# A four-layer convolution megakernel: filler products in TensorE's gaps, the last sums of one branch layer moved to VectorE, fewer TensorE taps in one chunk

## What is computed

```
x = x + L0(_gn(x))   # attention over the 4096 positions, softmax, value = key
x = x + L1(_gn(x))   # weights from a 128->16->9*128 net, 9 dilated taps: (wgt * patches).sum(axis=2)
x = x + L2(_gn(x))   # depthwise 7x7 (49 taps), layer norm over channels, 128->512 gelu ->128
x = x + L3(_gn(x))   # deformable 3x3 convolution, batch norm, relu
```

## Time and profile before

| | us |
|---|---|
| median of 3 runs | 4083.04 |
| the profiled execution, own time | 4088.41 |
| its span | 4086.7 |
| TensorE busy | 3426.9 |
| VectorE busy | 3225.1 |
| GpSimd busy | 2259.4 |
| ScalarE busy | 1954.3 |
| mean granted TensorE clock, share of full | 0.909 |

### The profile page before, as it was taken

How to read it: one execution, slowest core, us unless ns; L and a number is a source line. 1 busy time by engine, 2 the same in 40 slices (tenths; PEclk the granted TensorE clock), 3 DMA queues, 4 the chain that set the end, 5 groups by cost and what they waited for, 6 DMA issues and landing times. The chain is left out here.

```text
span 4086.7 us, 79072 instructions
## 1 busy us (share of the span) xinstructions
PE 3426.9 (84%) x28785; PEld 2168.6 (53%) x28785; DVE 3225.1 (79%) x6715; ACT 1954.3 (48%) x4385; POOL 2259.4 (55%) x2502
## 2 busy tenths in 40 slices
PE   4999968889999977979999976979999996883555
PEld 1666623447677742337767752335777762343444
DVE  5999867579999956659999957749999976755665
ACT  2444422346666632336666652345666653232333
POOL 3454550168878742038888835017887855006775
PEclk9999988989999988979999988989999998895556
DMA  1000002255555412055555521044555530127775
GB/s 50 9 12 12 27 16 51 66 154 149 154 154 148 125 37 50 1 170 153 151 150 152 150 61 43 8 129 142 156 152 146 155 95 18 44 63 209 220 218 175
DMA packets 219936, 426.59 MB, mean 104 GB/s; under 512 B 27825, under 2 KB 126540, under 8 KB 217512
## 3 DMA queue, kind: packets, MB, share of 16 engines
q0 software_dynamic: 92160, 302.06, 26.1%
q1 hardware_dynamic: 127346, 119.53, 10.2%
q10 hardware_dynamic: 54, 0.01, 0.0%
HBM read 340.77 MB, written 60.65 MB: 98 GB/s over the span
## 5 line engine op out<-in xcount | busy, mean ns | idle before, releaser
L1657 POOL TENSOR_TENSOR xl<-pt 128x192 bf16<-128x192 f32 (+1 forms) x1024 | 688.8, 674 | 425.0 <-PE bank L551 209.1
L878 ACT ACTIVATE pt<-bank 128x512 f32<-128x512 f32 x1024 | 608.8, 595 | 576.4 <-PE bank L520 344.9
L1646 POOL DMA_INDIRECT G<-patch_table,idx x576 | 593.9, 1031 | 162.8 <-issue 110.8
L551 PEld LDWEIGHTS bank<-vt,pt 128*128 128x128 bf16 x8192 | 550.0, 98 | 243.1 <-ACT pt L878 3.9
L1209 DVE TENSOR_REDUCE mxc<-bank 128x1 f32<-128x512 f32 x896 | 607.6, 679 | 37.4 <-PE bank L478 35.0
L551 PE MATMUL bank<-vt,pt 128*128 128x129 bf16 (+1 forms) x8192 | 634.3, 221 | 1.1 <-ACT osb L886 1.1
L1269 DVE TENSOR_TENSOR xl<-pt 128x320 bf16<-128x320 f32 (+1 forms) x1024 | 501.1, 490 | 72.3 <-PE bank L551 54.3
L551 PE MATMUL bank<-vt,xl 128*128 128x129 bf16 x4096 | 401.9, 221 | 12.7 <-DVE xl L1269 12.6
L1623 POOL TENSOR_TENSOR rs<-ve,mhalf 128x4 f32<-128x4 f32 x32 | 34.3, 1071 | 623.2 <-ACT ve L1005 623.2
L478 PE MATMUL bank<-reg,qh 128*128 128x512 bf16 x896 | 345.2, 386 | 12.0 <-DVE mxc L1209 8.5
L691 PE MATMUL bank<-reg,val 128*32 128x512 bf16 x3264 | 275.0, 399 | 65.4 <-DMA G<-xl 65.4
(11 more groups left out here) (248 smaller groups left out, 7020.2 us busy)
## 6 DMA issues: line engine op xcount, KB each, us to landing
patch_table<-valt SPq DMA_DIRECT2D x64, 512.0 KB, 7.0
G<-patch_table,idx POOLq DMA_INDIRECT x576
x_cur<-in_x SPq DMA_DIRECT2D x4, 2048.0 KB, 9.3
xl<-in_x SPq DMA_DIRECT2D x32, 256.0 KB
attn_out<-ob SPq DMA_DIRECT2D x32, 256.0 KB, 2.3
x_store<-x_cur SPq DMA_DIRECT2D x4, 2048.0 KB, 6.2
xr<-x_store SPq DMA_DIRECT2D x32, 256.0 KB
out<-fo SPq DMA_DIRECT2D x32, 256.0 KB
```

The costliest lines, as they stand in the source:

```text
L551: last = mm(O[t // 2][:, c0:c0 + width], image[:, at % ring, t * 128:(t + 1) * 128], vhl[:, values, st, 0:width], start=(st == 0 and part ...
L878: A(pt[:, at % PT_RING, :], ST[at % ST_RING] if n else ST_FIRST[at % 3], ACT.Exp, scale=SCALE).then_inc(s["exp_done"], 1)
L1646: g.indirect_dma_start(out=patches(j, k), out_offset=None, in_=table[:], in_offset=bass.IndirectOffsetOnAxis(ap=idx[:, j * K1 + k:j * K1 + ...
L1657: g.tensor_tensor(pl[:, at % PL_RING, 0:stop], pt[:, at % PT_RING, 0:stop], ph[:, at % PT_RING, 0:stop], ALU.subtract).then_inc(s["pl_p"], 1)
```

## The change

It has three parts. `keep_busy(bank, count)` lets TensorE multiply a constant (the bf16 identity) with another constant (512 columns of the layer-1 weights) `count` times, into a PSUM bank that nobody reads at that time; such calls are put around every group norm, behind the first products of layer 1 and in `step(8)` of layer 2. For the last chunk of layer 1 GpSimd keeps one addition alone and VectorE does the other three. In the first chunk of layer 2 TensorE does 27 taps in place of 34 and VectorE 22 in place of 15. In the diff the pieces stand in this order: TensorE (`keep_busy`, `layer1`, `layer2`, `sample`), VectorE (`layer1`, `layer2`), GpSimd (`layer1`).

```diff
-PE_TAPS = 34
+PE_TAPS, PE_TAPS_FIRST = 34, 27
...
+            def keep_busy(bank, count):
+
+                for _ in range(count):
+                    mm(P[bank], identb[:], l1w2_s[:, 0:CH // C, :], start=True, stop=True)
...
             def layer1(n):
...
                     mm(ST[c % 2][:], l1w1_s[:], rows(c), start=True, stop=True).then_inc(s["t_ps"], 1)
+                keep_busy(5, 20)
                 wait_alone(pe, s["tl_rdy"], NCH * n + 1)
...
                 def step(c, conv=True, norm=True, result=True):
...
+                    pe_taps = PE_TAPS if c else PE_TAPS_FIRST
...
                     if conv:
                         taps(12, 22)
+                    elif norm:
+                        keep_busy(2, 7)
...
-                        taps(25, PE_TAPS).then_inc(s["dwp"], 1)
+                        taps(25, pe_taps).then_inc(s["dwp"], 1)
+                    elif norm:
+                        keep_busy(2, 3)
...
             def sample(n, dcn):
+                if dcn:
+                    keep_busy(2, 18)
                 group_norm(4 * n)
+                if dcn:
+                    keep_busy(2, 8)
                 attention(n, dcn)
+                keep_busy(5, 50)
                 group_norm(4 * n + 1)
+                keep_busy(5, 8)
                 layer1(n)
+                keep_busy(5, 6)
                 group_norm(4 * n + 2)
+                keep_busy(5, 55)
                 layer2(n)
+                keep_busy(5, 6)
                 group_norm(4 * n + 3)
+                keep_busy(5, 28)
                 layer3_prepare(n)
...
                     if c >= 2:
                         stats(c - 2)
+                p, part = prod[(NCH - 1) % 3], pool_part[:, (NCH - 1) % 2, :]
+                dve.drain()
+                v.tensor_tensor(p[:, 4:6, :], p[:, 4:6, :], p[:, 6:8, :], ALU.add)
+                dve.drain()
+                v.tensor_tensor(p[:, 4, :], p[:, 4, :], p[:, 5, :], ALU.add)
+                dve.drain()
+                dve.wait_ge(s["l1x"], n + 1)
+                dve.wait_ge(s["l1a"], NCH * n + NCH - 2)
+                v.tensor_tensor(part, p[:, 4, :], p[:, 8, :], ALU.add).then_inc(s["l1s"], 1)
                 stats(NCH - 2)
                 stats(NCH - 1)
...
                 def step(c, u, conv=True, norm=True, result=True):
                     B = NCH * n + c
+                    pe_taps = PE_TAPS_FIRST if isinstance(c, int) and c == 0 else PE_TAPS
+                    dve_taps = KT - pe_taps
...
                     wait_alone(pool, s["l1p"], K1 // 3 * NCH * n + K1 // 3 * (c + 1) + 2)
+                    if c == NCH - 1:
+                        g.tensor_tensor(p[:, 8, :], p[:, 8, :], cols(x_cur, c), ALU.add).then_inc(s["l1x"], 1)
+                        break
                     g.tensor_tensor(p[:, 4:6, :], p[:, 4:6, :], p[:, 6:8, :], ALU.add)
```

More of the change, by code:

```diff
@@ L269, in build @@
             "st_rdy exp_done pl_v pl_p pv_done xst_rdy xft_ps xs_done xres_in o_evac ob_done r_out r_in "
-            "t_ps t_ev in_ve in_pow in_ready relu_rdy tl_rdy l1w l1p l1s l1a l1f "
+            "t_ps t_ev in_ve in_pow in_ready relu_rdy tl_rdy l1w l1p l1s l1a l1f l1x "
             "tapw_in tapw_rdy tapw_out tapw_ld im0 im1 im2 im3 dwp y_rdy ln_m ln_d ln_sq ln_v ln_ve ln_rs ln_dg ln_bc z_rdy hp gl mo me xa "
@@ L693, in taps @@
                                           shifted(c, k // 7 - 3, k % 7 - 3, stacked[j]),
-                                          start=(k == 0), stop=(k == PE_TAPS - 1))
+                                          start=(k == 0), stop=(k == pe_taps - 1))
                         return last
@@ L1384, in taps @@
                         for k in range(first, stop):
-                            tap = PE_TAPS + k
+                            tap = pe_taps + k
                             src = shifted(c, tap // 7 - 3, tap % 7 - 3)
@@ L1392, in taps @@
                                 v.scalar_tensor_tensor(acc, src, wgt, acc, ALU.mult, ALU.add)
-                            if k % 2 or k == DVE_TAPS - 1:
+                            if k % 2 or k == dve_taps - 1:
                                 dve.drain()
@@ L1402, in step @@
                     if conv:
-                        taps(7, DVE_TAPS)
+                        taps(7, dve_taps)
                     if norm:
```

## The result

| | before | after |
|---|---|---|
| median of the runs, us | 4085.91 (4 runs) | 4060.18 (4 runs, 4056.97 to 4062.42) |
| span of the profiled execution, us | 4086.7 | 4060.6 |
| mean granted TensorE clock | 0.909 | 0.937 |

The ratio of the times is 0.9938, with a 95% interval of 0.9920 to 0.9955: faster by 25.7 us, or 0.6%. The forecast was 35.8 us and 4047; the time lies in the range of 4026 to 4070.

The account below looks back on a forecast made before the run. Neither TensorE (84% busy) nor VectorE (79%) is saturated, so time is lost in hand-overs, with TensorE's clock falling in gaps. Terms 13.2 + 9.5 + 3.6 + 4.5 + 1.8 + 1.6 + 1.6 = 35.8 us off 4083.0 give 4047; range 4026 to 4070.

Parts of the forecast that it names:

- H: First group norm of samples 1 to 3: its 18 and 8 fillers fit and gain 0, at worst -0.8 us each.
- F: First products of layer 1: clock gain against 8 fillers pushing them back, -0.5 to +0.9, taken 0.4 each, 1.6 us in all.
- rival 3: Fillers run at the low level throughout and overrun their gaps: slower, 4176 us; chance 0.03.
- A: End of layer 1: earlier sums with VectorE held by GpSimd, faster last addition; 3.3 us a sample, 13.2 in all.
- B: First chunk of layer 2: 27 taps on TensorE, VectorE becomes the later one; 9.5 us in all.
- C: Second chunk of layer 2: TensorE's last nine taps at the high level; 0 to 1.9 each, 3.6 us in all.
- fourth rival: The gain is lost further on, to a transfer or to attention's start: 4083 us; chance 0.04.
- D: Step 8 of layer 2: seven fillers hold the clock for the MLP's second product; 1.5 in three samples, 4.5 us.
- E: Start of the weighting: six first products take 1.46 us in place of 2.72; 0 to 1.2 in three samples, 1.8 us.
- G: Behind the fourth group norm: 28 fillers overrun, but transposes and first taps run at the high level; +0.4 each, 1.6 us.
- Rival 2: The fillers change nothing, as the level falls in the gaps that remain: 11 us gain, 4072 us; chance 0.17.
- Rival 1: Everything runs at the high level and VectorE isn't held at layer 1's end: 51 us gain, 4032 us; chance 0.2.

Follow-up runs that it names:

- filling the wait: Changed kernel plus 14 fillers between first and second chunk of layer 2, in TensorE's wait for the second image: 4053.58 us, ratio 0.9928.
- the sample with the same wait: Second sample of the changed kernel run without the 18 and 8 fillers around the first group norm (samples 1 to 3): 4058.61 us, ratio 0.9933.
- one queue and 23 fillers: Changed kernel plus 14 fillers before layer 2's second chunk and 9 before its norm's last product, images on SP's queue only: 4041.96 us, ratio 0.9891.
- the first maxima: Two-queue kernel with more fillers, plus one filler behind each of 20 first-maxima products at the attention's start, samples 1 to 3: 4036.94 us, ratio 0.9887.
- the kernels with more fillers: Two image queues, 70 fillers for 55, 14 and 9 in layer 2's step 1, 20 at first maxima: 4036.94 us; with ten before layer 1's last addition: 4038.85.
- the experiment with two queues: Changed kernel with the second image's 16 transfers issued by ScalarE in place of SP: 4056.39 us, ratio 0.9936.

## Why the prediction was right, and where it was not

The direction and the range held; the size was too large by 10 us. That it was not 15 is luck: the 4.9 us of the attention (H) were not forecast and are not explained. Step by step:

- **The price of a filler** held: 55 took 12.03 us and 50 took 10.96, 0.22 each; where the level was low, 8 took 3.26, 0.41 each. The 28 outlast their gap, as forecast. So do the 8 behind the second group norm, which F had allowed for: the first product behind them starts 1.77 us after ScalarE begins `xn`, in place of 1.31. The large groups, 50 and 55, fit, so rival 3 did not come.
- **A** held in its mechanism. VectorE's first addition was held, and TensorE's wait fell from 5.20 to 2.78 us, by 2.4, where 2.3 was worked out for a held VectorE and 3.2 for a free one. The page of the Trainium skill named there (SBUF — State Buffer, "Who interferes with whom") says that the later of the two stands still until the earlier has ended. The trace agrees within 0.14 us: 1.94 us in place of 1.23, ending 1.09 us behind GpSimd. The second sample gained 10.18 - 6.83 = 3.35 us, forecast 3.3. In the other three the clock fell in the gap that is left, and they gained 2.4 to 2.6; this is the lower bound that was given (2.3, clock lost). Hence 10.8 in place of 13.2.
- **B** held: 10.6 against 9.5, and the wait at the first chunk's addition is 0.28 us. It was close: the first taps ran at the low level (0.61 us), and TensorE still ended after VectorE, by 0.1 to 0.4 us.
- **C is the step that failed.** The prediction took the second chunk's gain as "Between 0 and 1.9 each", and said that "the gain goes on", since the chunk starts with VectorE's low parts and taps. Its fourth rival brushed the matter aside: "The long waits of the list are for images, which move along." The first image does move along with the end of layer 1. The second follows the first by SP's 16 issues, 11.3 us later, and 34 taps had covered that almost exactly (1.12 us of waiting). A loss was left out of the bounds, and it was 2.3 us a sample. The trace of before held what was needed: the first taps of the two chunks begin, each with its image, at 1574.45 and 1586.07 (shown above), 11.6 us apart, and 27 taps were forecast to take 5.9 to 9 us. The prediction moved the chunk and did not count what SP's queue still had to issue for the next one. Undoing the taps (B +8.5, C -8.2) shows that the loss is the gain of the same part, moved; filling the wait (C -10.0), and the sample with the same wait in which the clock came back sooner (17.64 us), show that the clock lost in that wait made most of it. SP's pace by itself cost little: with one queue and 23 fillers C is 71.2 us, 7.6 below the kernel before. Whether 27 taps then beat 34 was not tested.
- **D** held: -1.70 us in each of samples 1 to 3, forecast 1.5. It is the clearest term: 24.9 us in each sample of the two kernels without fillers, 23.18 in each sample of all kernels with them.
- **E** was too high. The six first products take 1.46 us in place of 2.72 (they start at the high level, as hoped), but the stage lost only 0.8 us of the 4 x 1.26 = 5.0 that this could have given: they are mostly hidden.
- **F** and **G** are of the size forecast (1.9 against 1.6, and 1.0 against 1.6), in part by luck. F gained 0.8 and 1.0 us in the first two samples and 0.1 or less in the others; G gained 1.0, 0.9 and 0.4 in the first three and lost 1.4 in the last. The 28 fillers ran partly at the low level and took 7.9 us, the case that G priced as a loss; the first transposes gained 0.9 us all the same.
- **H**: the 26 fillers are worth nothing, as forecast. The attention was 4.9 us shorter none the less. In the kernels without fillers this stage took 2391.6 to 2395.2 us, in those with them (the first maxima left aside) 2385.9 to 2390.5. Which fillers do this, or whether it is scatter, stays open; it was only shown that it isn't the 26.
- **Rival 2** (fillers change nothing, 4072) is out: without them the kernel takes 4075, with them 4060. Its condition came true in part: the clock did fall in gaps that remain, in A and C. **Rival 1** (all at the high level, 4032) is what the kernels with more fillers come near to, 4037 and 4039. Its condition, no gaps of some 3 us left, is what they add.
- **The signs that it named.** VectorE's wait at the first chunk's addition, its held first addition and the 3.68 us of step 8 came. A clock near 1.00 up to the products of layer 1 and at the first taps of layer 2 did not (0.66 at 1470, 0.50 at 1566), and the last addition took about 1 us in one sample of four. Of the signs of being wrong two came: fillers at the low level (the 8, 0.41 us each), and a wait for the taps above 3 us, 3.29, though in the second chunk and not in the first.

## What to carry to other kernels

When a stage is shortened, look at what paces the stage behind it: here a queue that issues 16 small transfers at 0.63 us each set the distance between two images, and a chunk shortened below that distance won nothing, because the clock fell in the wait that this opened; with 23 fillers in its gaps, and the same queue, the second chunk took less than before. A filler pays where TensorE is the next to be waited for and the gap outlasts it; the same 14 products won 10 us in one place, and took back what nine others had won in another, because there the gap had closed. So place them by the idle time in front of each product, and read that again after every change to the order of arrival.

## What the runs showed of the hardware that was not expected

- The same gap in front of the last addition of layer 1, 2.75 to 2.78 us wherever it was read, left the clock at the high level in all eight samples of the two kernels without fillers (stage 6.80 to 6.82 us), and lowered it in three of four of the changed kernel (7.6 to 7.8 us). Ten products in the gap ended that. Why it falls with fillers elsewhere and not without stays open.
- Issuing is slow on either queue: 16 small transfers took 10.13 us on SP, 0.63 each, and in the experiment with two queues ScalarE's took 10.2 us for its own 16, 0.64 each.
- With the 28 fillers the stage behind the fourth group norm takes either about 42.8 or about 44.1 us in a sample (first three samples; once 45.5, with 9.12 us for the 28). Where they ran at the high level throughout they took 6.0 to 6.2 us and the stage 42.8 to 42.9; where it was low for a part of them, 7.15 to 7.89 us and 43.9 to 44.4. Which of the two comes is not decided by an edit near it, and differences of 4 us between kernels can come from there. Fewer than 28 were not tested.
